# The split of the next batch's x made two units later, and mix steps moved into the freed units

## The reference, cut to what matters

```python
w = weight[adapter_ids]                               # 2048x2048 for each batch
c = einsum('bsi,boi->bso', x, w)                      # the large product
c_norm = c * rsqrt(mean(c*c) + eps)
H_res  = sinkhorn_50(c_norm @ W_res.T + base)         # 4x4 for each token, 50 iterations
H_pre, H_post = softmax(c_norm @ W_pre.T + base), softmax(c_norm @ W_post.T + base)
H_res  = (1 - g) * I + g * H_res
y      = einsum('btnc,btn->btc', c_streams, H_pre) @ W_branch
out    = x + einsum('btij,btjc->btic', H_res, c_streams) + einsum('btc,btn->btnc', y, H_post)
```

## Time and profile before

| | us |
|---|---|
| median of 3 runs | 1774.47 |
| lowest, highest | 1774.23, 1777.13 |
| the profiled execution | 1779.6 |
| its span, first to last instruction | 1777.8 |
| PE busy in it | 1682.2 (95%) |
| DVE busy | 1488.3 (84%) |
| ACT busy | 709.5 (40%) |

### The profile page before, as it was taken

One profiled execution on the slowest core, in us unless ns is written; L12 is line 12 of the kernel. 1 busy time (PEld: TensorE's weight loads), 2 busy tenths in 40 slices (PEclk: granted clock), 3 DMA queues, 4 the chain that ended last, 5 costly groups with the idle time before them and its releaser, 6 DMA issues.

```text
span 1777.8 us, 24362 instructions
## 1 busy us (share of the span) xinstructions
PE 1682.2 (95%) x7690; PEld 1358.4 (76%) x7690; DVE 1488.3 (84%) x6016; ACT 709.5 (40%) x1143; POOL 95.8 (5%) x96
## 2 busy tenths in 40 slices
PE   9999999999999999999999999999999999999704
PEld 8888888877888788887888878887888878887601
DVE  4323599888999799987999889996999879997999
ACT  4334433343344534253343533344342543433503
POOL 0000000000000000000000000000000000000504
PEclk9999999999999999999999999999999999999857
DMA  6223323383244733475234832556234753347002
GB/s 231 93 93 132 131 95 107 107 256 135 95 120 149 233 104 107 107 209 176 90 106 120 261 129 84 128 167 213 97 107 112 212 174 95 107 135 233 1 1 94
DMA packets 65073, 237.72 MB, mean 134 GB/s; under 512 B 7344, under 2 KB 7472, under 8 KB 64816
## 3 DMA queue, kind: packets, MB, share of 16 engines
q1 hardware_dynamic: 56880, 206.80, 34.1%
q0 software_dynamic: 8064, 29.36, 9.2%
HBM read 202.58 MB, written 33.55 MB: 133 GB/s over the span
## 4 chain that ended last, share of the span: by engine, by line
PE 82%; DVE 13%; DMA 4%; ACT 1%; issue 0%; SPq 0%; ACTq 0%; DVEq 0%
PE acc L1016 71%; PE y_ps L1073 4%; DMA x_raw<-xt 3%; DVE piece L886 3%; PE turn_ps L1031 3%; DVE work L829 2%; DVE x_raw L912 2%; PE logit_ps L1039 2%; PE logit_ps L1042 2%; DVE vec L827 1%; DVE vec L825 1%; DVE x_lo L658 1%; DVE w_lo L650 1%; ACT x_hi L412 1%; PE y_ps L1063 1%; PE turn_ps L1051 0%
## 5 line engine op out<-in xcount | busy, mean ns | idle before, releaser
L1016 PE MATMUL acc<-w_hi,x_hi 128*128 128x512 f32 x2048 | 812.6, 397 | 3.7 <-ACT acc L428 2.7
L1016 PE MATMUL acc<-w_hi,x_lo 128*128 128x512 f32 x2048 | 799.5, 390 | 0.0
L1016 PE MATMUL acc<-w_lo,x_hi 128*128 128x512 f32 x2048 | 798.2, 390 | 0.0
L1016 PEld LDWEIGHTS acc<-w_hi,x_hi 128*128 128x128 f32 x2048 | 385.3, 188 | 85.5 <-issue 5.4
L1016 PEld LDWEIGHTS acc<-w_hi,x_lo 128*128 128x128 f32 x2048 | 384.9, 188 | 82.9
L1016 PEld LDWEIGHTS acc<-w_lo,x_hi 128*128 128x128 f32 x2048 | 385.6, 188 | 76.7
L405 ACT ACTIVATE w_hi<-w_raw 128x1024 fp32r<-128x1024 f32 x256 | 270.4, 1058 | 382.9 <-DMA w_raw<-wt 382.6
L650 DVE TENSOR_TENSOR w_lo<-w_raw,w_hi 128x1024 fp32r<-128x1024 f32 x256 | 311.7, 1218 | 108.9 <-ACT w_hi L405 108.2
L886 DVE SCALAR_TENSOR_TENSOR piece<-cond,kern,piece 128x512 f32<-128x512 f32 x448 | 304.1, 746 | 0.0
L829 DVE TENSOR_TENSOR work<-kern,vec 128x32 f32<-128x32 f32 x1536 | 250.5, 202 | 0.0
L827 DVE RECIPROCAL vec<-vec 128x8 f32<-128x8 f32 x1536 | 239.8, 198 | 0.0
(11 more groups left out here) (110 smaller groups left out, 799.0 us busy)
## 6 DMA issues: line engine op xcount, KB each, us to landing
w_raw<-wt SPq DMA_DIRECT2D x256, 512.0 KB, 3.5
x_raw<-xt SPq DMA_DIRECT2D x64, 512.0 KB, 6.1
piece<-xn POOLq DMA_DIRECT2D x56, 512.0 KB, 7.0
out<-piece SPq DMA_DIRECT2D x56, 512.0 KB, 4.7
x_raw<-xn SPq DMA_DIRECT2D x8, 512.0 KB, 6.3
out<-x_raw SPq DMA_DIRECT2D x8, 512.0 KB, 2.6
cond<-wb SPq DMA_DIRECT2D x1, 1024.0 KB, 15.4
cond<-wall SPq DMA_DIRECT2D x1, 192.0 KB, 13.4
```

The lines of the kernel that those rows point to most:

```text
L1016: mm = nc.tensor.matmul(acc[t][:], stationary, moving, start=(chunk == 0 and m == 0), stop=(chunk == CHUNKS - 1 and m == 2))
```

## The change

The next batch's places of x are split by a table of units, X_AT, two units later than before: place u in unit 28+u, so places 0 to 3 in units 28 to 31, place 4 in the next batch's unit 0, place 5 in its unit 1, and places 6 and 7 both in its unit 2. The loads by SP stay where they are. In units 26 and 27 there is one mix step more each, in unit 34 (the next batch's unit 2) two fewer. Piece 5 is spread in unit 26 instead of 27. As the mix steps of pieces 4 and 5 end a unit sooner, SP's stores of them stand a unit sooner as well.

```diff
+X_AT = {28: (0,), 29: (1,), 30: (2,), 31: (3,), 32: (4,), 33: (5,), 34: (6, 7)}
-SPREAD_AT = (14, 14, 19, 19, 25, 27, 28, 29)
+SPREAD_AT = (14, 14, 19, 19, 25, 26, 28, 29)
-MIX_AT = {21: 1, 22: 3, 23: 3, 24: 3, 25: 3, 26: 3, 27: 2, 28: 2, 29: 3, 30: 2, 31: 3, 33: 1, 34: 3}
+MIX_AT = {21: 1, 22: 3, 23: 3, 24: 3, 25: 3, 26: 4, 27: 3, 28: 2, 29: 3, 30: 2, 31: 3, 33: 1, 34: 1}
+        def x_units(b, U, end):
+
+            units = [(b, u) for u in X_AT.get(U + UNITS, ())] if end else []
+            return units + [(b + 1, u) for u in X_AT.get(U, ()) if b < BATCHES - 1]
-                    if end and U < 2:
-                        x_high(b, PASS_UNITS - 2 + U)
-                    if not last and U >= 3 * PASS_UNITS + 2:
-                        x_high(b + 1, U - 3 * PASS_UNITS - 2)
+                    for place in x_units(b, U, end):
+                        x_high(*place)
-                    if not last and U >= 3 * PASS_UNITS + 2:
-                        x_low(b + 1, U - 3 * PASS_UNITS - 2)
                     if not end:
+                        for place in x_units(b, U, end):
+                            x_low(*place)
                         continue
-                    if U < 2:
-                        x_low(b, PASS_UNITS - 2 + U)
+                    for place in x_units(b, U, end):
+                        x_low(*place)
```

## The result

The changed kernel took 1764.68 us (median of 4 runs, 1763.09 to 1767.02) against 1775.8 for the kernel before (4 runs, 1774.23 to 1779.25): a ratio of 0.9936, 95% interval 0.9916 to 0.9956. That is 11.1 us less, where 15.5 were forecast. The time lies outside the forecast's own range (1755.5 to 1762) and inside the wider one, 1755.5 to 1768, that counts rival A.

What follows compares the result with a forecast made beforehand. PE, busy 1682.2 of 1777.8 us, was taken as the bound. Gain: 14.4 us of waits plus 1.7 of clock less 0.6 remainder, 15.5; 1774.5 - 15.5 = 1759.0 us, own range 1755.5 to 1762, wider range 1755.5 to 1768.

Steps and rivals of the forecast that it cites:

- rival A: Batch boundary: a late transfer, piece 6's load or unit 1's weights, keeps some gain away; 1766 or 1764 us; 13%.
- Its sign: Rival A's sign in the profile: DVE waits 2 us or more for piece 6's load, projection's wait still there.
- The ten waits: PE at batch boundaries: six for DVE's transposed block, four for ACT's accumulator; 14.4 us in all, to go.
- the two falls of the clock: Behind the projection's two longest waits: granted clock 0.50 for 3.4 us each, costing 3.4 us together.
- The cause: Boundary loop between DVE and SP: mix steps delay a store, then place 4's x load, making ACT and DVE late.
- Units 0 to 2 of the next batch: Unit 2: two x_lo (2.28 us) replace two mix steps (2.66); DVE reaches the next Sinkhorn 0.4 us sooner.
- The new wait: DVE in unit 29 waits 0.8 us for the load into piece 6, leaving 0.3 us to spare.
- I take 8.1 us and no PE wait: Piece 6's load in unit 29 lands after 8.1 us, from bounds 5.2 to 10.3, costing PE nothing.
- The reserve of 1.1 us: Unit 0's transposed block: DVE starts it at 814.33, needed at 815.44, so 1.1 us to spare.
- A's other half: Unit 1's weights come as late as now: PE waits 0.9 us, 5.4 in all, giving 1764 us; within A's 13%.
- it comes sooner: Unit 31: w_hi of unit 1 comes sooner, place 4's load being out of its way; otherwise DVE is 2.0 us late.
- half of 3.4 us: Clock's share in the median forecast: 1.7 us, since whether the median's run had falls was open.

Runs made afterwards that it cites:

- SP's order alone: Kernel before, with SP issuing the next batch's x load ahead of the store in each unit: 1766.31 us, ratio 0.9961.
- the halves: Kernel before with only x's split moved: 1776.5 us, ratio 1.0; with only mix steps and spread moved: 1769.4 us, ratio 0.9957.
- the first trace: Profiled execution of the changed kernel in the first comparison, no further edit: 1767.02 us.
- the repeated run: Changed kernel measured again without edit, beside other runs on one chip: 1763.51 us, ratio 0.9925 to the kernel before.
- x alone: Kernel before with only x's split two units later: 1776.5 us, ratio 1.0; also with nine Sinkhorn pairs moved later: 1764.31 us, ratio 0.995.
- mix steps alone: Kernel before with only the mix steps and the spread moved, x split where it was: 1769.4 us, ratio 0.9957.

## Why the prediction was right, and by how much it was off

**In short**: the place of the loss, its size and its cause were right. The outcome is not the forecast, which had 77%, but rival A, which had 13%: 1764.68 lies above the forecast's own range and near A's 1764 to 1766. Its sign showed too, DVE's wait for the load at 2 us or more at two boundaries with the projection's wait still there.

**The bound and the place of the loss**: right. The ten waits and the two falls of the clock were nearly the whole of what the loop could give: when all of them are gone the profiled span is 1759.8, 18.0 us less than 1777.8, where 17.8 were worked out. By the length of PE's units it is 18.6, so the 0.16 us added to each wait was a little short.

**The cause**: right as a chain and confirmed one link at a time, by SP's order alone (8.8 us by the medians) and by the halves. But I priced the parts as if x carried the gain and the moved mix steps only a cost. The halves give 0.6, 7.7 and together 13.6 us on one chip. The mix steps are worth more than half by themselves, as they let the store end sooner, and they make x's move worth anything.

**"Units 0 to 2 of the next batch"**: the direction was right and its weight wasn't seen. DVE comes to the start of the Sinkhorn work (line 773, 769 before) 1.4 us ahead of PE's unit 4, before the change 0.6 (0.9 us sooner, where 0.4 was reckoned). Without the two mix steps that leave unit 2 it comes 1.2 us behind, and that costs six waits of 1.6 us.

**The new wait**: seen, and mis-sized; this is the step that failed. "I take 8.1 us and no PE wait: it is this very load, and its neighbours change in its favour, since the store of piece 4 has left SP's unit 29" had the sign of the neighbours wrong. What leaves with the store is the hold on the load of place 4, which now comes 0.3 us behind this load instead of 2.9. The load took 8.1 to 10.7 us, where it had taken 7.8 to 8.1 before, and the run with SP's order alone, 8.8 to 9.6, shows the same by itself. So DVE waited 0.7 to 3.3 us, not 0.8. The reserve of 1.1 us was mis-sized as well (0.8), and did not hold at three boundaries in the first trace. PE paid 3.3 us in them as the rows show it, 4.1 by the length of its units, and 1.5 once for the clock. Rival A's price, 1764 to 1766, fits the median, though it came of fewer and larger waits than its six of 1.2 us. Its chance should have been more, with 0.3 us left over against loads of this kind that ranged from 5.2 to 10.3.

**A's other half**: in the changed kernel unit 1's weights let ACT start at 3.4 to 5.4 us ahead of the boundary, against 3.6 before; "it comes sooner" was worth 1.7 us at best. The Trainium skill's rule (DMA: Bandwidth & Descriptors, Queues, rings and completion order), that a DMA engine takes turns between its queues, was the better guide. The traces agree: only with a load of the other queue moved away did they come some 3 us sooner. It cost little by itself in the changed kernel: at the second boundary of the repeated run ACT evacuates late behind these weights, and PE waits 0.4 us for the accumulator. In the runs with x alone it was what the boundary still cost.

**The clock**: one fall of two stayed, to a granted clock of 0.5, behind a wait shown as 2.01 us; the ten later traces have none in the loop after its first 30 us. The length of one wait does not decide it: the two falls before came behind waits shown as 1.83 and 1.90 us, while waits of 1.82 (before), 1.78 (mix steps alone) and 1.92 us (x loaded first) left the clock alone. I took half of 3.4 us in the median. The scatter of the kernel before (1771.28 to 1780.17 in 17 runs on one chip) is wider than two falls can make, against 0.8 us in six runs of the changed kernel. So the clock alone does not scatter it; that landings of loads do is my reading, not shown.

**Left open**: why the second boundary is the worst in six of the ten traces that have waits. Transfers there are slow together: the weights of unit 0 took 8.5 us in the changed kernel and place 4 took 11.8, against 3.7 to 5.0 and 5.7 to 9.7 at the other five.

## What to carry to other kernels

When a store waits for compute and a load stands behind it in the same queue, late compute makes the load late and the load makes compute late; look in the chain of waits for compute, store, load, compute in a ring, and put the load first. Before moving work past a boundary, follow the engine that takes it until its next idle time, with everything it owes another engine on the way, and take the lead from the one that is needed soonest, not from the most frequent one. When a load is freed to start sooner, ask which load it now starts beside. A reserve smaller than a transfer's own scatter is no reserve: give the transfer one more unit.

## What the hardware showed that I had not expected

The load that adds x to a piece, 512 KB by POOL, took 8.2, 9.4 and 10.7 us at three boundaries of one execution with the same program around it. A load of x by SP issued 0.3 us behind it instead of 2.9 made it some 1 us slower (8.8 to 9.6 us against 7.8 to 8.1). Issued 1.9 us later, it landed 0.7 us later in the mean of six boundaries, from 0.5 sooner to 1.7 later. A weight load of 512 KB took 3.4 to 3.6 us with no such load about, 3.9 to 6.4 beside one and 6.5 to 9.1 beside two, in the changed kernel and its versions with one of the two moved. The kernel before, with waits at six boundaries, scatters from run to run by 8.9 us in 17 runs, 14.7 in 20 and 5.8 in 11 on three chips; the kernel with piece 6 spread sooner, without any, by 1.8 in 6.
